# A layernorm's normalisation written by ScalarE, with its bias made by GpSimd

## The reference

```
def _layernorm(x, axis=-1, eps=1e-05):
    m = jnp.mean(x, axis=axis, keepdims=True)
    v = jnp.var(x, axis=axis, keepdims=True)
    return (x - m) / jnp.sqrt(v + eps)
...
x = x + tanh(g_xattn[0]) * retention(_layernorm(x), ctx)          # layer 0
x = x + tanh(g_ffn[0])   * top1_of_8_experts(_layernorm(x))       # layer 1
x = x + tanh(g_xattn[1]) * grouped_causal_attention(_layernorm(x), ctx)
x = x + tanh(g_ffn[1])   * sparse_2to4_ffn(_layernorm(x))
```

## Time and profile before

| | us |
|---|---|
| median of 3 runs (lowest, highest) | 408.97 (408.11, 408.98) |
| the profiled execution, its time | 409.77 |
| the profiled execution, its span | 407.7 |
| TensorE busy in the span | 343.9 |
| VectorE busy | 214.6 |
| ScalarE busy | 160.1 |
| GpSimd busy | 98.2 |

### The profile page before, as it was taken

How to read it: one execution, slowest core, us unless ns; L and a number is a source line. 1 busy time by engine, 2 the same in 40 slices (tenths; PEclk the granted TensorE clock), 3 DMA queues, 4 the chain that set the end, 5 groups by cost and what they waited for, 6 DMA issues and landing times.

```text
span 407.7 us, 4563 instructions
## 1 busy us (share of the span) xinstructions
PE 343.9 (84%) x1477; PEld 206.9 (51%) x1477; DVE 214.6 (53%) x509; ACT 160.1 (39%) x336; POOL 98.2 (24%) x148
## 2 busy tenths in 40 slices
PE   2999785519999848989799989979889879999997
PEld 1485564406665526545454555444443434444886
DVE  5134985601232248879446934881241338679921
ACT  2443221204333123145873875477873223333000
POOL 7102543430000346301340442054450001000000
PEclk9999998558999656999999999998999999999999
DMA  7995000143111115400000000000000000000011
GB/s 214 382 424 110 1 13 2 45 151 115 54 39 53 39 47 172 195 6 0 9 0 2 0 6 2 0 2 8 0 2 0 0 2 0 0 0 2 13 51 39
DMA packets 13879, 22.40 MB, mean 55 GB/s; under 512 B 2033, under 2 KB 11249, under 8 KB 13042
## 3 DMA queue, kind: packets, MB, share of 16 engines
q1 hardware_dynamic: 13090, 20.03, 14.4%
q0 software_dynamic: 768, 2.10, 1.6%
HBM read 15.83 MB, written 6.03 MB: 54 GB/s over the span
## 4 chain that ended last, share of the span: by engine, by line
PE 58%; DVE 19%; ACT 8%; issue 7%; POOL 4%; DMA 3%; SPq 0%; DVEq 0%; ACTq 0%; POOLq 0%
PE bank L229 43%; DVE mx L1150 8%; PE bank L438 5%; ACT region L874 5%; PE bank L406 3%; DVE stats L945 2%; POOL x_sorted L691 2%; PE bank L409 2%; PE bank L242 1%; POOL rstd L667 1%; DVE x_sb L985 1%; ACT qst L825 1%; PE bank L452 1%; DMA x_sb<-in_x_dram 1%; PE bank L486 1%
## 5 line engine op out<-in xcount | busy, mean ns | idle before, releaser
L1150 DVE TENSOR_REDUCE mx<-bank 128x2 f32<-128x512 f32 (+1 forms) x96 | 59.8, 684 | 14.0 <-PE bank L409 14.0
L874 ACT ACTIVATE region<-bank,padcol 128x512 f32<-128x512 f32 x96 | 60.8, 701 | 12.6 <-PE bank L229 11.6
L729 POOL TENSOR_SCALAR_AFFINE_SELECT region<-region 128x1024 f32<-128x1024 f32 x32 | 35.0, 1094 | 94.6 <-ACT region L874 94.3
L229 PE MATMUL bank<-xT,e_gu 128*128 128x512 f32 x128 | 56.6, 594 | 0.5 <-ACT xT L746 0.5
L229 PE MATMUL bank<-qst,kblk 128*128 128x512 f32 x96 | 46.1, 507 | 1.6 <-ACT region L874 0.7
L406 PE MATMUL bank<-kblk,qst 128*128 128x512 f32 x96 | 43.3, 475 | 1.6 <-DVE mx L1150 0.9
L229 PEld LDWEIGHTS bank<-xT,e_gu 128*128 128x128 f32 x128 | 23.8, 190 | 28.0 <-issue 27.1
L663 POOL TENSOR_SCALAR veps<-mv 128x1 f32<-128x1 f32 x40 | 11.3, 283 | 80.5 <-DVE mv L947 80.1
L409 PE MATMUL bank<-causb,identb 128*128 128x256 bf16 (+1 forms) x96 | 30.6, 319 | 0.0
L746 ACT ACTIVATE xT<-bank 128x256 f32<-128x256 f32 x32 | 12.4, 386 | 44.1 <-PE bank L236 43.9
L229 PE MATMUL bank<-e_down,region 128*128 128x256 f32 x128 | 27.8, 379 | 0.0
(11 more groups left out here) (155 smaller groups left out, 557.0 us busy)
## 6 DMA issues: line engine op xcount, KB each, us to landing
e_gu<-in_e_gu_dram SPq DMA_DIRECT2D x2, 1408.0 KB, 12.6
x_sorted<-zero SPq DMA_DIRECT2D x1, 1920.0 KB, 10.3
y_sorted<-region SPq DMA_DIRECT2D x15, 128.0 KB, 1.7
x_sb<-in_x_dram SPq DMA_DIRECT2D x4, 256.0 KB, 4.0
ctxT<-in_ctxT_dram SPq DMA_DIRECT2D x2, 512.0 KB, 7.6
e_down<-in_e_down_dram SPq DMA_DIRECT2D x1, 1024.0 KB, 13.6
region<-x_sorted SPq DMA_DIRECT2D x1, 1024.0 KB, 7.4
e_gu<-in_f_gate_dram SPq DMA_DIRECT2D x1, 1024.0 KB, 4.8
```

What stands on the lines that cost most here:

```text
L229: return pe.matmul(dst, lhsT, rhs, start=first, stop=last)
L729: pool.affine_select(out=block, in_=block, compare_op=ALU.is_ge, fill=0.0, base=0, pattern=[[0, 2], [0, PER_GROUP], [1, P]], channel_multi ...
L874: taken(act.activation(dst, src.rearrange("p (h n) -> p h n", n=SEQ - mt * P), ACT.Exp, bias=padcol[:, key:key + 1], scale=float(HD) ** -0 ...
L1150: taken(dve.reduce_max(mx[:, b % 2, nt, quads, q, hg], src, AX), "sa")
```

## The change

The eight normalisations of the second layernorm go from VectorE to ScalarE, as x * rstd + shift by an activation of the kind Identity, with scale and bias read from SBUF. GpSimd makes shift = mean * rstd * -1 for each tile, behind the tile's rstd, after a wait for it. In ScalarE's round k the new instruction stands for tile k-2, behind the copy of the transposed product and before the copy of the transposed layernorm of tile k-3.

```diff
+        shift = sb("shift", [P, TILES])
...
                 if k >= 3:
                     inverse_std(1, k - 3, LN_EPS)
+                    pool.wait_ge(sem("rstd1"), k - 2)
+                    pool.tensor_scalar(shift[:, k - 3:k - 2], mv[:, 1, k - 3, 0:1], rstd[:, 1, k - 3:k - 2], -1.0,
+                                       ALU.mult, ALU.mult).then_inc(sem("shift"), 1)
...
                     taken(act.activation(actT[:, k % 2, :, :], src[:, 0:DIM].rearrange("p (t n) -> p t n", t=KT),
                                          ACT.Copy), "wyT")
+                if 2 <= k < TILES + 2:
+                    tile = HALF_ORDER[k - 2]
+                    act.wait_ge(sem("shift"), k - 1)
+                    act.activation(xn1[:, tile, :], x_sb[:, tile, :], ACT.Identity, bias=shift[:, k - 2:k - 1],
+                                   scale=rstd[:, 1, k - 2:k - 1]).then_inc(sem("xn1"), 1)
                 if k >= 3:
                     ln_turn(1, k - 3)
...
                 if k + 1 < TILES:
                     gn_scale(k + 1)
-                if k >= 2:
-                    norm(1, k - 2)
                 if 1 <= k <= TILES:
                     residual("res0", k - 1, 0)
```

## The result

The changed kernel takes 405.86 us (median of 6 executions, 405.14 to 407.36) against 409.15 (6 executions, 408.11 to 410.38) of the kernel before on the same chip: ratio 0.992, 95% interval 0.9897 to 0.9944. That is 3.3 us faster; 405.0 was forecast, with a range of 404.0 to 406.5. The profiled execution took 406.18 us with a span of 404.1, against 409.77 and 407.7. Two of the 13 executions of the kernel before that stand beside e5 to e8 were slow (578.35 and 834.66 us) and are in no ratio.

The account below looks back on a forecast made before the run. VectorE was taken to bound four steps, then one chain through the tail and routing; 1.2 + 0.96 + 1.0 + 0.8 = 4.0 us won, from the 408.97 us median to 405.0 us, range 404.0 to 406.5.

Parts of the forecast that it names:

- rival (a): Tail of the stage: TensorE's clock falls all the same, so the clock gain is gone; 405.8 us, chance 0.12.
- term 4: Last transposes to copy of the logits: TensorE's clock stays at 2.4 GHz until the logits are done, winning 0.8 us.
- Term 1: Four full steps: without the normalisation on VectorE each falls from 3.22 to 2.92 us, winning 1.2 us.
- Term 2: Last tile's residual on VectorE: no longer behind the seventh normalisation, it starts once its projection is there, winning 0.96 us.
- Term 3: Last normalisation, in the tail: on ScalarE it is not held up by GpSimd's clears, winning 1.0 us.
- The open point: Last normalisation: if the clears held ScalarE up too, its term would be -0.5 us instead of 1.0.
- What I said costs nothing: GpSimd's and ScalarE's added work is covered in the 2.92 us steps; waiting copies cost at most 0.1 us, clears 0.3.
- (c): Start of the experts, at 90 us: something else ends last there, so nothing is won; 409.0 us, chance 0.06.
- (d): Full steps and tail: GpSimd becomes the bound and the kernel gets slower, 411.9 us at a 2.0 us instruction; chance 0.06.

Follow-up runs that it names:

- e5: Changed kernel plus three unused matmuls in TensorE's two tail pauses (two, then one): 406.14 us, ratio 0.9932.
- e8: Changed kernel with the last normalisation back on VectorE, GpSimd's clears behind it, and two unused matmuls in TensorE's first tail pause: 404.82 us, ratio 0.991.
- e11: The changed kernel itself, unaltered, measured and profiled a second time: 407.36 us, ratio 0.9935 to the kernel before.
- e2: Changed kernel with only the first seven normalisations on ScalarE, the last one on VectorE: 406.77 us (one execution).
- e3: Kernel before, all normalisations on VectorE, with only GpSimd's two clears made to wait for the last normalisation: 407.82 us, ratio 0.9971.
- e4: Changed kernel plus seven unused matmuls in TensorE's two tail pauses (four, then three): 405.74 us, ratio 0.9909.
- e12: The changed kernel itself, unaltered, profiled a third time: 405.70 us (one execution).
- e6: Changed kernel with GpSimd's new instruction made twice for each tile, the first result unused: 406.89 us (one execution).
- e9: Kernel before plus one spare GpSimd instruction of the new one's form, for the first tile only, result unused: 408.19 us (one execution).
- e10: Kernel before plus one spare GpSimd instruction with only an immediate operand and one operation, result unused: 408.47 us (one execution).

## Why the prediction was right, and where it was not

The time, 405.86 us, lies in the range, 0.9 us above the forecast of 405.0. It is the time of rival (a), 405.8, and by luck: rival (a) leaves out term 4 and knows nothing of the 0.37 us below. The second measurement of the same kernel, 407.36 us in e11, lies above the range, with the kernel before only 0.5 us higher than in the first (409.61 against 409.15).

**Term 1 (1.2 us; 1.22 measured)** was right by its own reason: the steps are 2.92 us, with VectorE and the loop through TensorE within hundredths of each other (in the step from 46.23 us the projection ends at 48.01, and VectorE, busy till then, starts the residual at 48.05), and e2 has them with the last normalisation on VectorE as before.

**Term 2 (0.96; 0.96 measured)** was right: the residual was late for no other reason than its place in VectorE's order.

**Term 3 (1.0; 0.94 measured)** was right in mechanism. Its parts in the tail: GpSimd's instruction 0.27 us for 0.28 forecast, ScalarE's 0.60 for 0.56, starting 0.40 us after the last power's end. The open point, whether ScalarE too would be held up beside the clears, is settled by its 599 to 601 ns; that the clears held VectorE up is shown from the other side by e3. This agrees with the exclusive port pair of VectorE and GpSimd in the Trainium skill (SBUF — State Buffer, "Who interferes with whom"): the clears start at 65.84 us, VectorE's normalisation at 65.93, and it ends at 67.83, behind both of them.

**Term 4 (0.8; 0 in the profile that was compared)** is the step that failed. I argued that the clock falls after a long pause and that a short pause is safe. Three profiles of one program show the fall 2.1, 2.8 and 5.0 us after the start of one and the same pause of 1.21 us, with work behind it. So neither the length of the last pause nor the program decides alone; the fall was to be taken as a chance, and half of 0.7 us into the sum. The program does shift that chance: by the mean clocks the fall of e4 is late in four of four executions, and seven of ten of e3 have 0.941, which the changed kernel never reaches. Rival (a), at 0.12, was put too low. Two more points were off. The pause of 1.21 us is not in the prediction, which counts only the last one (0.6 us forecast, 0.74 measured); the same transposes waited for 0.66 us in the kernel before:

```profile
64.01 0.41 PE L236 MATMUL bank<-ident,region 128*128 128x128 f32 x2 [0.66 <-DVE region L957]
```

And even where the clock stood, in e12, the term is 0.66 us and not 0.8: from ScalarE's last copy (65.28 us) to VectorE's reading (66.37) it takes 1.09 us, for 0.95 forecast.

**What I said costs nothing** did cost nothing, though not as I had it. In the full steps GpSimd's instruction took 0.49 us and not 0.28, beside VectorE's centring (L1009), and ScalarE, which I said would not stand still, waited 0.33 us for it:

```profile
47.24 0.48 DVE L1009 SCALAR_TENSOR_TENSOR region<-region,mv,gamma 128x256 f32<-128x256 f32 x1
47.36 0.49 POOL L679 TENSOR_SCALAR shift<-mv,rstd 128x1 f32<-128x1 f32 x1
...
47.89 0.60 ACT L785 ACTIVATE region<-x_sb,shift,rstd 128x256 f32<-128x256 f32 x1 [0.33 <-POOL shift L679]
```

The cover was wide enough for it: GpSimd had room for twice the load (e6), the copies on ScalarE behind the waiting instruction delayed nothing that TensorE waited for later than the last tile, and the clears ended at 65.51, before the copy of the logits at 66.72.

**Not foreseen:** 0.37 us between the routing and the scatter, which come with one more small instruction on GpSimd and its tensor and semaphore (e9, e10). I had written that the scatter follows the routing as it is. This gain stands in for about half of the missing term 4; without it the time would lie nearer 406.2 us. Rivals (c) and (d) have nothing for them: the win of the tail arrives at the experts whole (86.59 against 90.48 us).

## What to carry to other kernels

Where an instruction in the tail takes several times as long as its like, look at what the other engines do in the same microseconds before moving it to another engine: here putting two clears behind it took 1.5 us off the path of the tail with one wait (e3). An in-order queue is to be read for what stands behind each wait; the residual behind a normalisation cost 0.96 us without either engine being busy. A gain that rests on the clock at one moment should be priced by several profiles of the same program, not by one.

## What the runs showed of the hardware

The moment at which the granted clock falls in a stretch of sparse work differs between executions of one program by more than 2 us measured from the same matmul (5.0 in e12 against 2.1 in the first profile; worked out from the mean clock of the 1 us windows). The start of an indirect DMA on GpSimd moved by 0.37 us (1.41 to 1.04) with one small instruction more, 30 us ahead of it, together with its SBUF tensor and its semaphore; which of the three does it is open. A small GpSimd instruction that runs beside a VectorE instruction with two SBUF inputs was itself stretched (0.27 to 0.50 us) and left VectorE's at 0.48, while GpSimd's two clears (1.84 us together) stretched a VectorE instruction with one SBUF input from 0.41 to 1.90 (e3 against the kernel before).
